# One stream of expert chunks through the attention and the stage of a 16-image conv, attention and mixture-of-experts kernel

## What is computed

```
x = x + conv_block(group_norm(x))           # row and column state scans, gated mix
t = tokens(x)                               # 16 x 1024 tokens of 192
t = t + attention(layer_norm(t))            # 6 heads of 32, window 33 and one CLS token
scores = layer_norm(t) @ gate_w + gate_b    # 4 experts, the best 2 of softmax(scores)
h = gelu(layer_norm(t) @ w1[e] + b1[e])     # 192 -> 768, exact gelu
t = t + sum over the 2 experts of gate[e] * (h @ w2[e] + b2[e])
x = image(t)
```

## Time and profile before

| | us |
|---|---|
| median of 3 runs | 3410.94 (3409.24 to 3419.26) |
| span of the profiled execution | 3590.9 |
| attention of image 10 | 82.1 |
| stage of image 10 (24 chunks) | 123.2 |
| PE, busy share of the span | 82% |
| DVE, busy share | 53% |
| ACT, busy share | 30% |
| POOL, busy share | 23% |

### The profile page before, as it was taken

One profiled execution on the slowest core, in us unless ns is written; L12 is line 12 of the kernel. 1 busy time (PEld: TensorE's weight loads), 2 busy tenths in 40 slices (PEclk: granted clock), 3 DMA queues, 4 the chain that ended last, 5 costly groups with the idle time before them and its releaser, 6 DMA issues.

```text
span 3590.9 us, 51454 instructions
## 1 busy us (share of the span) xinstructions
PE 2939.1 (82%) x18691; PEld 2073.7 (58%) x18691; DVE 1890.2 (53%) x5214; ACT 1060.1 (30%) x3287; POOL 814.0 (23%) x656
## 2 busy tenths in 40 slices
PE   0587777888889888888989888988978888897677
PEld 0455555656556565656656565665656565665444
DVE  4563545545554555545555555655555455544444
ACT  0142323232323323232322323232332323233222
POOL 0000111231312223131212213122222313122424
PEclk9697878989999798989979898998989899998889
DMA  3320103232222323123232312322232322323365
GB/s 42 102 69 13 54 14 83 59 78 49 49 78 53 89 54 91 41 53 90 42 80 54 90 55 43 88 42 85 52 87 59 81 47 48 79 51 82 94 161 114
DMA packets 272636, 241.86 MB, mean 67 GB/s; under 512 B 209020, under 2 KB 250494, under 8 KB 261760
## 3 DMA queue, kind: packets, MB, share of 16 engines
q1 hardware_dynamic: 211648, 147.17, 15.4%
q0 software_dynamic: 50880, 52.59, 9.1%
q10 hardware_dynamic: 9856, 38.80, 3.4%
HBM read 133.29 MB, written 73.59 MB: 58 GB/s over the span
## 4 chain that ended last, share of the span: by engine, by line
PE 52%; DVE 19%; another core or an unknown queue 4%; issue 4%; ACT 3%; SPq 2%; POOL 1%; DMA 1%; DVEq 0%; POOLq 0%
PE PSUM L1449 9%; PE PSUM L1426 6%; PE PSUM L1518 5%; PE PSUM L1496 4%; PE PSUM L1467 3%; PE PSUM L1435 3%; PE PSUM L1469 3%; PE PSUM L1468 3%; DVE NMX L1064 3%; SPq L558 2%; PE PSUM L1389 2%; ACT HF L774 2%; DVE HLO L1012 1%; PE PSUM L1588 1%
## 5 line engine op out<-in xcount | busy, mean ns | idle before, releaser
L803 ACT ACTIVATE PSPT<-PSUM,NMX 94x126 f32<-94x126 f32 x1056 | 366.1, 357 | 660.0 <-DVE NMX L1064 331.0
L1449 PE MATMUL PSUM<-XT,WB 128*128 128x512 f16 x2010 | 512.4, 386 | 43.6 <-DMA META<-slots 43.6
L679 POOL DMA_INDIRECT out_dram<-Y,META x228 | 360.9, 1583 | 708.9 <-DVE Y L1036 516.1
L1009 DVE TENSOR_SCALAR HHI<-HF 128x512 f16<-128x512 f32 x402 | 176.4, 439 | 607.2 <-ACT HF L774 600.2
L774 ACT ACTIVATE HF<-PSUM,WB 128x512 f32<-128x512 f32 x402 | 276.0, 687 | 706.6 <-PE PSUM L1449 704.9
L1467 PE MATMUL PSUM<-WB,HHI 128*128 128x192 f16 x1608 | 403.3, 251 | 19.3 <-DVE HLO L1012 17.8
L1469 PE MATMUL PSUM<-WB,HLO 128*128 128x192 f16 x1608 | 402.7, 250 | 0.0
L1468 PE MATMUL PSUM<-WB,HHI 128*128 128x192 f16 x1608 | 402.5, 250 | 0.0
L1496 PE MATMUL PSUM<-KBD,QT 128*94 128x378 f32 x704 | 358.2, 597 | 18.8 <-ACT PSPT L803 17.2
L635 POOL TENSOR_TENSOR TR<-TV,MHALF 128x4 f32<-128x4 f32 (+1 forms) x48 | 59.4, 1238 | 1359.6 <-DVE TV L887 1359.6
L1518 PE MATMUL PSUM<-VW,PSPT 126*94 126x32 f32 x2112 | 248.8, 272 | 130.3 <-DVE PSPT L1046 104.8
(11 more groups left out here) (267 smaller groups left out, 4820.1 us busy)
## 6 DMA issues: line engine op xcount, KB each, us to landing
WB<-weights SPq DMA_DIRECT2D x67, 1600.0 KB
XR<-in_x ACTq DMA_DIRECT2D x16, 768.0 KB, 5.3
out_dram<-X ACTq DMA_DIRECT2D x32, 384.0 KB, 2.4
weights<-WB ACTq DMA_DIRECT2D x4, 1600.0 KB, 6.2
GUP<-TGU SPq DMA_DIRECT2D x256, 8.0 KB, 1.8
slots<-XROW,IDX POOLq DMA_INDIRECT x256
out_dram<-Y,META POOLq DMA_INDIRECT x228
HF<-in_w ACTq DMA_DIRECT2D x6, 384.0 KB, 4.7
```

What stands on the lines that cost most here:

```text
L679: pool.indirect_dma_start(out[:, :], bass.IndirectOffsetOnAxis(row, 0), Y[:, wslot(i, j), q, :], None, bounds_check=B * T + BS - 1, oob_is ...
L803: e = act.activation(PS[0:QS, n % 2, h, :], PSUM[0:QS, n % 2, h * KS:(h + 1) * KS], ACT.Exp, bias=NMX[:, b, n % 2, h:h + 1], accum_out=DEN ...
L1449: mm = pe.matmul(dst, WB[:, ws, w:w + 128], XT[:, xs, chunk, :], start=(n == 0), stop=(n == 4))
```

## The change

The chunks of all 67 blocks become one stream, numbered by g, that every engine advances wherever it likes. A stage runs 10 chunks instead of 24. The other 14 run in the next attention: one in each of its twelve passes and two in what follows them, in the places of `keep_busy`, from attention 3 on (`filled`). In an attention's pass PE puts `ffn1` between the scores and `turn`, and `ffn2` of the chunk before between `turn` and `values`; ACT puts the Gelu behind the pass's exponentials; DVE puts `split` between `copy_turned` and `normalize`. In the stage each chunk is followed by four or five steps of `rest` and `conv`. Since a schedule is now still read while the next is made, `PICK` and `SCHED` have two copies. The stage of image 15 runs 84 chunks, and the last dispatch is chained to `rest(15)` beside them. The prefix sum moves from bank 4 to bank 3, and the attention's output projection from banks 4 and 5 to 2 and 3. The queues of SP and POOL are rewritten to fit: the adds of an image's later blocks move into the next attention, behind its scatter, and SP takes a block's tokens and weights later.

```diff
+ATTN_CHUNKS = 14
-        PICK = sb("PICK", [128, NSEL_END, E])
+        PICK = sb("PICK", [128, 2, NSEL_END, E])
-        SCHED = sb("SCHED", [128, NSEL_END, 2], I32)
+        SCHED = sb("SCHED", [128, 2, NSEL_END, 2], I32)
...
+        def filled(i):
+            return i > 2
...
-        STEPS = [(1, n % 2) if n < 17 else (2, 1) for n in range(NSEL * HK)] + [(1, 1)]
+        STAGE_CHUNKS = NSEL * HK - ATTN_CHUNKS
+        STEPS = [(3, 2) if n % 2 else (2, 2) for n in range(STAGE_CHUNKS)]
+        def stage_chunks(i):
+            return HK if i == 1 else STAGE_CHUNKS if i < B - 1 else NSEL * HK + NSEL_END * HK
...
# SP
+            for i in range(2, B):
+                g = first_block(i)
+                if i > 2:
+                    expert(g - 1)
+                selected(i)
+                tokens(g)
+                tokens(g + 1)
+                expert(g)
+                if not last(i):
+                    state_moves(i + 1)
+                expert(g + 1)
+                tokens(g + 2)
+                tokens(g + 3)
+                expert(g + 2)
# ACT
                         e.then_inc(s["exp_done"], 1)
+                    if filled(i):
+                        step((stream,), 2)
+                step((stream,), 2 if filled(i) else 0)
                 for n in (0, 2):
                     evacuate_oT(act, n, i)
...
                 act.activation(CW[:], CW[:], ACT.Exp).then_inc(s["cls_exp"], 1)
+                step((stream,), 2 if filled(i) else 0)
...
                 turned_tokens(i, 1)
+                step((stream,), 2 if filled(i) else 0)
# DVE
                         copy_turned(2 * b - 2)
                         copy_turned(2 * b - 1)
+                    if filled(i):
+                        step((stream,), 2)
+                    if b >= 1:
                         normalize(b - 1)
...
                 dve.wait_ge(s["x2b_free"], at("x2b_free", i, 1))
+                step((stream,), 2 if filled(i) else 0)
...
                 norm_tokens(X2, range(4, 8)).then_inc(s["xn2_ready"], 1)
+                step((stream,), 2 if filled(i) else 0)
                 token_rows(i, 1)
...
+            def stage(i, *side):
                 step(side, STEPS_AHEAD)
+                for n in range(stage_chunks(i)):
+                    step((stream,), 2)
+                    step(side, sum(steps_at(n)))
                 finish(side)
...
-            experts(B - 1, rest(B - 1))
-            gates(B)
-            positions(B)
-            schedule(B, last_blocks=True)
-            experts(B)
+            stage(B - 1, chain(rest(B - 1), dispatch_last()))
+            block_out(BLOCKS - 1)
# PE
+            def fill(i, idle, at_bank=5):
+                if filled(i):
+                    next(stream)
+                else:
+                    keep_busy(idle, at_bank)
...
                     if following and b == 3:
                         group_variance(i + 1)
+                    fill(i, 0)
                     if b >= 1:
                         turn(2 * b - 2)
+                        if before and b == 3:
+                            pe.wait_ge(s["slots_ready"], at("slots_ready", i, 0))
...
+                    fill(i, 8 if b == 1 else 2)
                     if b >= 1:
-                        keep_busy(8 if b == 1 else 2)
                         values(2 * b - 2)
                         values(2 * b - 1)
...
-                keep_busy(5)
+                fill(i, 5)
```

More of the change, by code:

```diff
@@ L42 @@
 W_A, W_2H, W_2L, W_B2, W_B1 = 0, 3840, 4992, 6144, 6336
-LINKS_0, LINKS_1, LINKS = 72, 67, 73
+ATTN_CHUNKS = 14
 X_UP, W_UP, H_UP = 1024.0, 64.0, 8.0
@@ L691, in image @@
                     conv_states(i + 1)
-                if not first(i):
-                    add(i, 0)
+                if i >= 2:
+                    add(g - 1)
                 if not last(i):
                     conv_tokens(i + 1)
-                if not first(i):
-                    for j in range(1, blocks_of(i)):
-                        add(i, j)
+                    if i >= 2:
+                        add(g)
             rstd(0, GR[:], GV[:], 2, "gn_eps", "gn_rstd")
@@ L1039, in block_out, with chunks @@
                                       (128, 2, 2, C)), ALU.mult).then_inc(f["y_ready"], 1)
+            def chunks():
+                for g in range(BLOCKS):
+                    for k in range(HK):
+                        yield
+                        if g and k == 1:
+                            block_out(g - 1)
+                        if k == 2:
+                            block_gates(g)
+                            if picked_in(g) == B:
+                                block_rows(g)
+                        split(g, k)
+                        yield
+            stream = chunks()
             def attention(i):
@@ L1239, in rest, with stage, dispatch_last @@
                 yield
-            def experts(i, *side):
+            def stage(i, *side):
                 step(side, STEPS_AHEAD)
-                for n in range(blocks_of(i) * HK):
-                    j, k = divmod(n, HK)
-                    if n > 1 and k == 1 and j:
-                        block_out(i, j - 1)
-                    if k == 2:
-                        block_gates(i, j)
-                        if isinstance(i, int) and i == B:
-                            block_rows(j)
-                    split(i, j, k)
-                    step(side, sum(STEPS[n % len(STEPS)]))
-                block_out(i, blocks_of(i) - 1)
-                finish(side)
+                for n in range(stage_chunks(i)):
+                    step((stream,), 2)
+                    step(side, sum(steps_at(n)))
+                finish(side)
+            def dispatch_last():
+                yield
+                yield
+                gates(B)
+                yield
+                yield
+                positions(B)
+                yield
+                schedule(B, last_blocks=True)
+                yield
             def split_weights(n):
@@ L1470, in ffn2, with chunks @@
                 mm.then_inc(f["ffn2_chunk"], 1)
+            def chunks():
+                for n in range(BLOCKS * HK + 1):
+                    if n < BLOCKS * HK:
+                        ffn1(*divmod(n, HK))
+                    yield
+                    if n:
+                        ffn2(*divmod(n - 1, HK))
+                    yield
+            stream = chunks()
+            def fill(i, idle, at_bank=5):
[3 more added lines that the diff above has]
+                    keep_busy(idle, at_bank)
             def prefix(i):
@@ L1642, in _ @@
             finish((rest(0), conv(1)))
-            attention(1)
-            experts(1, rest(1), conv(2))
-            for i in range(2, B - 1):
+            for i in range(1, B - 1):
                 attention(i)
-                experts(i, rest(i), conv(i + 1))
+                stage(i, rest(i), conv(i + 1))
             attention(B - 1)
-            experts(B - 1, rest(B - 1))
-            prefix(B)
-            experts(B)
+            stage(B - 1, chain(rest(B - 1), dispatch_last()))
+            finish((stream,))
 def kernel(**inputs):
```

294 lines of the change are left out of this document (148 added, 146 removed).

## The result

The changed kernel takes 3893.25 us (3883.02 to 3895.01, median of 4 runs) against 3410.09 us (3405.47 to 3419.26, 4 runs) of the kernel before on the same chip: a ratio of 1.141, with a 95% interval from 1.139 to 1.143. The forecast of 3501 us had the sign, but the loss is 483 us and not 90; the range ended at 3620.

A forecast was written before the change was run, and what follows sets the result against it. It took an ACT and DVE loop of 6.4 us to set the changed attention's pass, over PE's 5.41. Attention +32 and stage -22, thirteen times, gave +130; the end -40; 3410.9 + 90 = 3501 us, range 3350 to 3620.

The forecast's parts named there:

- the sign: Whole kernel: slower, by 90 us; slower by more than about 0.3% was given 0.70.
- The second load: Attention pass, ACT: the load after the Gelu runs beside 2.0 us of DVE work and costs nothing.
- The quiet pass: Attention: a pass without other DVE work goes from 3.83 to 6.4 us, a loop closed over DVE's next maximum.
- Loads: Attention: one 1.30 us load per pass lies on the loop, giving 6.4 us where PE alone needs 5.41.
- The clock: Attention: no term in the sum; one more spell at 1.2 GHz would make its growth 37 us instead of 32.
- The stage: Stages of images 2 to 14: losing 14 of 24 chunks saves 22 us each, between 16.6 and 29.0.
- The base: Attention before the change: ten passes took 61.8 us, including an 8.75 us remote wait left in both sums.
- The end: After image 15's stage: dispatch, scatter and loads hide beside 84 chunks, 40 us less, between 47 and none.
- The loop hides its load: Attention: PE sets the pass at 5.41 us, attention grows by 21, total 3358 us; chance 0.20.
- The stage gives back the full price: Stage: 29 us saved per image, total 3410 us, no change; chance 0.10.
- Each switch costs twice its row: Attention: ACT also empties before loads behind exponentials, 1.30 us more per pass, total 3683 us; chance 0.05.
- The end hides nothing: After image 15's stage: the 40 us are not given back, total 3541 us; chance 0.10.

The follow-up runs named there:

- the run with the early table: Changed kernel plus a one-element exponential on ACT behind each Gelu of an attention, waiting for nothing of the pass: 3814.1 us.
- the kernel without loads: Changed kernel with the experts' Gelu replaced by Tanh, which shares the exponential's table, so no table is loaded in an attention: 3581.2 us.
- the second profile: The kernel before, unedited, profiled again: span 3413.2 us, with no DVE wait for anything remote.
- the timed runs of the filler: Changed kernel with Tanh for Gelu, plus filler matmuls in filled attentions where PE stood empty: 3469.9 us, against 3581.2 us without that filler.
- the two runs of the end: Kernel before with only the last dispatch beside the 84 last chunks: 3486.5 us; again, with stages finishing their own last chunk and output: 3383.6 us.

## Why the prediction was wrong

**The step that failed** is the sentence "The second load runs on ACT while DVE splits, normalizes and takes the maximum (2.0 us), so it costs nothing as long as these take more than 1.30." The engine was free, but the instruction was not: it waited for PE's `turn`. The quiet pass came out at 7.80 us instead of 6.4. The loop closes over that `turn` and not over the next maximum, but this changed its length little: with one load it is what the run with the early table shows, 6.52. A second step failed nearly as badly: the sum has no term for the clock that falls where filler is taken away. The sign came out right since an attention lost more than a stage gave back; the range was missed by 273 us.

From +90 to +483 us, term by term:

- **Loads.** They cost an attention 128.2 - 104.7 = 23.5 us. The forecast charged 6.4 - 5.41 = 1.0 for each of eleven passes and one load behind them, about 12. Missing: 11.5 x 13 = 150.
- **The clock.** The forecast's middle had nothing for it, its range one spell of 5 us. In the kernel without loads the filler gave back 104.7 - 94.9 = 9.8 an attention. Missing: 9.8 x 13 = 127 (111 in the timed runs). The sum weighed filler as PE time that a chunk replaces; that it also kept PE from standing empty was left out.
- **The stage.** 22 was taken between bounds of 16.6 and 29; 17.0 came. Missing: 65. The low bound, from image 1's stage, was nearly exact (1.21 us a chunk against 1.19): chunks there fill waits of the conv, and taking them out leaves the waits. PE is idle for 20.8 us of image 10's stage now, at a clock of 0.90, and for 10.8 of image 13's before, at 0.99.
- **The base.** With 8.75 us of remote waiting left in both sums, ten passes were counted as 53.0 us. From the first maximum to the last they are 49.1 in the second profile, averaged as above: that execution had more remote waits than the one. Missing: 3.9 x 13 = 51.
- **The end.** -31.7 instead of -40. Not 7 us but about 11 stay empty, 4.52 ahead of the prefix sum, 2.11 behind it and 4.09 ahead of the first chunk of the last ten blocks, and the clock falls behind the first and in the last of them. Missing: 8.

Together 401 us, where the forecast was short by 392; with the timed runs of the filler, 385. They fit no closer than that, since the clock was priced in a kernel without loads.

**The rivals.** *The loop hides its load* is refuted by 7.80. But its number for PE, 5.41, was good: 5.10 without loads. And its sum would not have held even so: with neither loads nor a low clock, 14 chunks cost an attention 94.9 - 71.6 = 23.3 us and give the stage back 17. *The stage gives back the full price* is refuted by 17.0. *Each switch costs twice its row* forecast a pass of 7.7 and was the nearest number, but by luck: its mechanism, ACT emptying itself between exponentials and load, is refuted by the gap of 0.01 us. *The end hides nothing* is refuted by the two runs of the end.

**What would show it.** Two table loads for each chunk and DVE idle behind the first were there. Attentions near 114 and passes of 6.4 were not. That stages came out near 106 and not 101 was within what the text allowed.

## What to carry to other kernels

A table load is not free work that an engine does when it has time: it has a place in the list, and here that place was behind a wait of its function (510.6 us of idle ACT). So look in the trace for the wait that releases the load. Here a call that waited for nothing brought the load forward, and a quiet pass from 7.80 to 6.52 us. Halving the switches, with two chunks' Gelus behind one load, was not tried. And before work is put where filler stood, ask what kept PE going there: here work that itself waited did not replace filler, and a pass behind the wait ran at half the clock (11.72 us against 8.18). Last, a profile longer than the timed runs should be read for waits that belong to that execution alone, before its stretches become terms of a sum.

## What was not expected of the hardware

The exponential's load had 2.33 us of idle ACT ahead of it and did not use them (130 waits, 510.6 us in all). And, in the kernel without loads, 64 matmuls more in each attention made it 111 us faster: the fourth pass took 11.72 us at a clock of 0.50, and 8.18 at 1.00 with 16 more matmuls in it. That a load waits with one of its function's waits and runs ahead of another was not expected either.
